# Routing four turns at once in a fused mixer and gated-expert kernel on one core of Trainium2

## The reference, cut to what matters

```python
xn = layernorm(x)                        # 16 sequences x 256 tokens x 128 channels = 4096 tokens
# mixer, per sequence: six projections of x + (prev - x) * mix
state = state * decay + u                # a scan over 256 tokens
mn = groupnorm(r * state)                # 16 groups of 8 channels
s = (mn * gn_w + gn_b) * g @ W_out.T + b_out
# experts: four rounds over the same tokens
for r in range(4):
    logits = cur @ Wg[r] + bg[r]
    vals, idx = top_k(logits, 2);  w = softmax(vals)      # of 4 experts
    y = gelu(cur @ W1[e] + b1[e]) @ W2[e] + b2[e]         # all four experts, 128 -> 512 -> 128
    cur = cur + sum_e cw[e] * y[e]
out = x + s * silu(cur)
```

## Time and profile before

| | us |
|---|---|
| median of 3 runs | 899.56 |
| the profiled execution, its own time | 899.89 |
| its span in the trace | 898.0 |
| TensorE matmul busy | 814.8 (91%) |
| VectorE busy | 808.4 (90%) |
| ScalarE busy | 647.8 (72%) |
| chain that ended last, by engine | PE 49%, DVE 31%, ACT 10%, issue 9%, DMA 1% |

### The profile page before, as it was taken

The page is one execution under the profiler, slowest core; times in us unless marked ns, Lnnn a source line. Parts: engine busy times, 40 slices in busy tenths (PEclk is TensorE's granted clock), DMA queues, the critical chain, the costliest instruction groups (busy, mean ns, idle before and its releaser), DMA issues.

```text
span 898.0 us, 12889 instructions
## 1 busy us (share of the span) xinstructions
PE 814.8 (91%) x3640; PEld 646.8 (72%) x3640; DVE 808.4 (90%) x1756; ACT 647.8 (72%) x900; POOL 146.8 (16%) x167
## 2 busy tenths in 40 slices
PE   3889999889899999999999999999999999898994
PEld 2667777767687777778777777877777787676873
DVE  8899999988989989898998989899898989998894
ACT  3656767767687777768777777877777787676872
POOL 5011241421111111111111111111111111111111
PEclk7799999999999999999999999999999999998997
DMA  7132344323444333334333343433333354533453
GB/s 208 48 82 36 83 89 86 77 44 82 95 88 88 82 54 76 82 94 94 82 82 68 67 86 84 94 82 86 80 60 79 82 118 95 129 58 72 119 118 82
DMA packets 40458, 76.58 MB, mean 85 GB/s; under 512 B 6384, under 2 KB 18800, under 8 KB 36336
## 3 DMA queue, kind: packets, MB, share of 16 engines
q0 software_dynamic: 18432, 33.56, 21.7%
q1 hardware_dynamic: 21808, 42.69, 16.9%
q10 hardware_dynamic: 192, 0.01, 0.0%
HBM read 40.33 MB, written 2.36 MB: 48 GB/s over the span
## 4 chain that ended last, share of the span: by engine, by line
PE 49%; DVE 31%; ACT 10%; issue 9%; DMA 1%; DVEq 0%; ACTq 0%; POOLq 0%
PE h_bank L734 8%; PE h_bank L733 8%; PE h_bank L732 8%; DVE g_lo L517 7%; PE y_bank L765 6%; PE y_bank L770 6%; PE y_bank L766 6%; ACT g L341 6%; ACT g_hi L345 4%; DVE lgt L481 2%; DVE xm L573 2%; DVE xm_lo L581 2%; DVE tmp L528 2%; PE r_bank L742 1%; DVE xm_hi L579 1%
## 5 line engine op out<-in xcount | busy, mean ns | idle before, releaser
L341 ACT ACTIVATE g<-h_bank,b_c 128x512 f32<-128x512 f32 x512 | 333.3, 680 | 126.2 <-PE h_bank L734 121.4
L517 DVE TENSOR_TENSOR g_lo<-g,g_hi 128x1024 fp32r<-128x1024 f32 x256 | 306.7, 1223 | 40.5 <-ACT g_hi L345 37.8
L345 ACT ACTIVATE g_hi<-g 128x1024 fp32r<-128x1024 f32 x256 | 271.6, 1061 | 8.1
L309 POOL DMA_DIRECT2D cur<-tmp x128 | 111.3, 870 | 734.8 <-DVE tmp L528 506.9
L732 PE MATMUL h_bank<-cur_lo,w_hi 128*128 128x512 f32 x512 | 210.3, 411 | 0.0
L733 PE MATMUL h_bank<-cur_hi,w_lo 128*128 128x512 f32 x512 | 207.1, 404 | 0.0
L734 PE MATMUL h_bank<-cur_hi,w_hi 128*128 128x512 f32 x512 | 206.6, 404 | 0.0
L765 PE MATMUL y_bank<-g_hi,w_hi 128*128 128x512 f32 x512 | 203.0, 396 | 0.0
L766 PE MATMUL y_bank<-g_hi,w_lo 128*128 128x512 f32 x512 | 202.2, 395 | 0.0
L770 PE MATMUL y_bank<-g_lo,w_hi 128*128 128x512 f32 x512 | 140.4, 395 | 0.1
L734 PEld LDWEIGHTS h_bank<-cur_hi,w_hi 128*128 128x128 f32 x512 | 99.1, 194 | 24.4
(11 more groups left out here) (110 smaller groups left out, 671.3 us busy)
## 6 DMA issues: line engine op xcount, KB each, us to landing
cw_b<-cw_scratch SPq DMA_DIRECT2D x32, 1024.0 KB, 5.8
cur<-tmp POOLq DMA_DIRECT2D x128, 256.0 KB, 3.3
cur<-in_x SPq DMA_DIRECT2D x8, 256.0 KB, 5.1
xr<-in_x SPq DMA_DIRECT2D x8, 256.0 KB, 6.6
out<-o SPq DMA_DIRECT2D x8, 256.0 KB, 6.0
g<-in_w SPq DMA_DIRECT2D x4, 256.0 KB, 5.4
cw_scratch<-cw SPq DMA_DIRECT2D x32, 8.0 KB, 1.4
cw_b<-in_proj_t SPq DMA_DIRECT2D x1, 384.0 KB, 3.4
```

What stands on the lines that cost most here:

```text
L309: pool.dma_start(cur[:, ds((s // E % NB) * BLK, BLK)], tmp[:, t % 2, :], accum_op=ALU.add).then_inc(summed, DMA)
L341: nc.scalar.activation(g[:, gb, ft * BLK:(ft + 1) * BLK], hb[ft][:, :], ACT.Gelu_apprx_tanh, bias=b1_c[:, e * FT + ft:e * FT + ft + 1]).th ...
L345: nc.scalar.activation(g_hi[:, gb, h], g[:, gb, h], ACT.Copy).then_inc(g_hi_done, 1)
L517: nc.vector.tensor_tensor(g_lo[:, gb, h], g[:, gb, h], as_f32(g_hi[:, gb, h]), ALU.subtract).then_inc(g_lo_done, 1)
```

## The change

- **Router.** Turns 0 to 7 are routed one by one as before. The turns from 8 on are routed four at a time, in passes 3, 5, 7, 9, 11 and 13: `logits_four` runs eight matmuls at t = 4 into all 128 partitions of `r_bank`, two per turn. Its weights are windows of `wg_pad`, which is zero but for 8 columns, so that turn n of the four adds its scores to partitions 32n to 32n + 31 and zeros to the others. One `router_scores` (t = 5) and one `router_gates` (t = 6) then work on 128 partitions. Passes 4, 6, 8, 10, 12, 14 and 15 have no router; pass 3 has one for turn 7 at t = 1 and 2, and the first of four at t = 5 and 6.
- **Splits.** `cur_hi` and `cur_lo` have five buffers. From pass 4 to 13 the splits lie at t = 1 and t = 3, two turns further ahead; pass 3 has four of them; passes 14 and 15 have none. A split now waits for `up_done` of the turn whose buffer it takes.
- **Banks.** The transposes of `mixed` and `mn` go to `p_bank` and wait for `p_empty`.
- **Gates.** The transfer of a turn's gates now waits in the SyncE queue for the last `combine` of the turn before the previous one as well, since the gates of four turns are ready together.
- **Loops.** `Fori` is gone: all passes are written out, and semaphore counts are constants.
- Some buffers are merged (`mixed` with `st`, `gated` with `gn`, `z` with `th`, `xn_st` with `o`), `wg_now` is gone, and two small fills make the zeros of `wg_pad` before pass 0.

```diff
-        cur_hi, cur_lo = sb("cur_hi", [128, 2, BLK], f32r), sb("cur_lo", [128, 2, BLK], f32r)
+        cur_hi, cur_lo = sb("cur_hi", [128, SPLITS, BLK], f32r), sb("cur_lo", [128, SPLITS, BLK], f32r)
...
-        lgt = sb("lgt", [RP, RT, RP])
+        lgt = sb("lgt", [128, RT, RP])
...
+        def routed(i):
+
+            return SPLIT_PASSES <= i <= TAIL_PASS and i % 2 == 1
...
+        def splits_at(i, t):
+
+            if norming(i):
+                return {3: (2 * i + 2,), 7: (2 * i + 3,)}.get(t, ())
+            if i == SPLIT_PASSES:
+                return {1: (2 * i + 2, 2 * i + 3), 3: (2 * i + 4, 2 * i + 5)}.get(t, ())
+            if i <= TAIL_PASS:
+                return {1: (2 * i + 4,), 3: (2 * i + 5,)}.get(t, ())
+            return ()
...
-                sp.wait_ge(cw_ready, k + 1)
+                q, n = k % 2, batch_of(k)
+                row = RP * (k % QUADS if k >= NB else 0)
+                sp.wait_ge(cw_ready, n + 1)
+                if k >= 2:
+                    sp.wait_ge(combined, 2 + E * (k - 1))
...
+            def split_cur(k):
+
+                off, q = k % NB * BLK, k % SPLITS
+                if k >= NB:
+                    dve.wait_ge(summed, DMA * E * (k - NB + 1))
+                if k >= SPLITS:
+                    dve.wait_ge(up_done, E * FT * (k - SPLITS + 1))
...
-            def mixer_norm(i, job):
-
-                dve.wait_ge(r_full, job + 1)
-                m3 = rb[:, 0:2 * D].rearrange("p (g c) -> p g c", c=GW)
+            def mixer_norm(i):
+
+                dve.wait_ge(p_full, JOBS * i + J_MIXED + 1)
+                m3 = pb[:, 0:2 * D].rearrange("p (g c) -> p g c", c=GW)
...
+            def turn_mixer(i, job, src, ready):
+
+                pe.wait_ge(ready, i + 1)
+                pe.wait_ge(p_empty, JOBS * i + job)
+                for t in range(2):
+                    ins = nc.tensor.transpose(pb[:, t * D:(t + 1) * D], src[:, t * D:(t + 1) * D], ident[:, :])
+                ins.then_inc(p_full, 1)
...
+            def logits_four(k, job):
+
+                pe.wait_ge(r_empty, job)
+                for n in range(QUADS):
+                    pe.wait_ge(cur_split, 2 * (k + n + 1))
+                    w = wg_pad[:, WG_AT - RP * n:WG_AT - RP * n + 128]
+                    q = (k + n) % SPLITS
+                    nc.tensor.matmul(rb[:, :], w, cur_lo[:, q, :], start=(n == 0), stop=False)
+                    last = nc.tensor.matmul(rb[:, :], w, cur_hi[:, q, :], start=False, stop=(n == QUADS - 1))
+                last.then_inc(r_full, 1)
```

More of the change, by code:

```diff
@@ L174, in mixer_gated_experts, with norming, ending, kinds_of @@
         GATEW, SMALL, MIXW = 2, 4, 2
[L179 to L182, removed]
-        R_BEFORE = 3
[L184 to L192, removed]
+        J_RW, J_AG, J_KV, J_MIXED, J_MN, J_S = range(6)
+        JOBS = 6
+        def norming(i):
+            return i < SPLIT_PASSES
+        def ending(i):
+            return i >= TAIL_PASS
+        def routed(i):
+            return SPLIT_PASSES <= i <= TAIL_PASS and i % 2 == 1
+        def kinds_of(i):
+            kinds = []
+            if i < SPLIT_PASSES:
+                kinds += ["logits_odd", "norm_even", "logits_even", "norm_odd"]
+            if i == SPLIT_PASSES:
+                kinds += ["logits_odd"]
+            if ending(i):
+                kinds += ["end_even"]
+            if routed(i):
+                kinds += ["logits_four"]
+            if ending(i):
+                kinds += ["end_odd"]
+            if i == PASSES - 1:
+                kinds += ["end_6"]
+            return kinds
+        R_BEFORE = 3
+        r_jobs = {}
+        for i in range(PASSES):
+            for name in kinds_of(i):
+                r_jobs[i, name] = R_BEFORE + len(r_jobs)
+        r_jobs[PASSES - 1, "end_7"] = R_BEFORE + len(r_jobs)
         def end_job(b):
@@ L251, in store @@
                              o[:, b % 2, :].rearrange("p (t d) -> p t d", t=TPB)).then_inc(stored[b % 2], DMA)
[L253 to L256, removed]
+            spread_gates(0)
+            for i in range(TAIL_PASS):
+                spread_gates(2 * i + 1)
+                spread_gates(2 * i + 2)
             for i in range(TAIL_PASS, PASSES):
@@ L404, in _ @@
             act.wait_ge(lo_split, 2 * E)
-            passes(act, one_pass)
+            for i in range(PASSES):
+                one_pass(i)
             end_tanh(NB - 1)
@@ L410, in _ @@
             class Own:
[L412 removed]
+                n = 0
             def link(ins):
@@ L719, in _ @@
[L719 to L722 removed]
+                    if t == 1 and i <= SPLIT_PASSES:
+                        router_scores(2 * i + 1, r_jobs[i, "logits_odd"])
+                    elif t == 2 and i <= SPLIT_PASSES:
+                        router_gates(2 * i + 1)
+                    elif t == 5 and norming(i):
+                        router_scores(2 * i + 2, r_jobs[i, "logits_even"])
+                    elif t == 5 and routed(i):
+                        router_scores(2 * i + 2, r_jobs[i, "logits_four"])
+                    elif t == 6 and (norming(i) or routed(i)):
+                        router_gates(2 * i + 2)
@@ L724, in _ @@
+                    combine(i, t)
+            for i in range(PASSES):
+                one_pass(i)
             end_output(NB - 2, end_job(NB - 2))
-            dve.wait_ge(p_empty, 4 * PASSES)
+            dve.wait_ge(p_empty, JOBS * PASSES)
             end_product(NB - 1)
@@ L837, in _ @@
             pe.wait_ge(lo_split, 2 * E + 2)
-            passes(pe, one_pass)
+            for i in range(PASSES):
+                one_pass(i)
             turn(end_job(NB - 1), z[:, 1, :], TPB, z_ready, NB)
```

335 lines of the change are left out of this document (158 added, 177 removed).

## The result

| | before | after |
|---|---|---|
| median, us | 899.19 (4 runs) | 863.04 (862.53 to 863.11) |
| ratio | | 0.9595 (95%: 0.9576 to 0.9614) |
| profiled execution, us | 899.89 | 862.53 |
| its span, us | 898.0 | 860.7 |
| granted clock, mean | 0.972 | 0.981 |

The change makes the kernel 4% faster. The forecast was 861.7 us. (A fourth execution of the changed kernel took 2798.85 us and is left out of the ratio and the range; the median of all four is the 863.04 above, that of the other three 862.96.)

The account below looks back on a forecast made before the run. TensorE was taken as the bound, less two stalls where VectorE is late (VectorE in passes 0 and 1). Gains 0.2 + 2.4 - 0.8 + 24.9 + 2.4 + 7.8 + 1.3 = 38.2 us off 899.89 gave 861.7; range 852 to 876.

Parts of the forecast that it names:

- pass 3: Pass with both routers and four splits: 52.0 us against 51.2, `xm_lo` stall 1.5 and `go_lo` 1.15, a loss of 0.8.
- passes 4 to 12: Loop passes: even ones 47.9 us, odd ones 50.9 with a 1.15 us `go_lo` wait, 443.1 against 468.0, gain 24.9.
- pass 14: No router there: two stalls of 4.2 us and 2.66 of low clock go, scores save 0.93; 48.7 us, gain 7.8.
- Router on 128 partitions: VectorE's router calls: 128 partitions at the price of 32, up to 1 us more allowed; load falls 7.7 and 3.8 us.
- Wider weight loads: TensorE's score matmuls: 128-column loads of 0.194 us against 0.087 cost nothing, covered by the matmul before.
- The copies to `wg_now` go and two fills come: Passes 0 and 1, bound by VectorE and keeping their routers: a few tenths either way, gain 0.2 us.
- At least 22 us: Gate transfers: start at least 22 us before they are wanted and land within about 8, so cost nothing.
- Loops cost nothing: Loop branches: priced at nothing, as 49.15 us busy and 2.85 of named waits fill a 52.0 us pass.
- A: Rival, odd passes: router chain hidden, six TensorE stalls of 1.15 us go, 853 to 855 us; chance 0.13.
- B: Rival: VectorE late at more places, even passes keep a 1.2 to 2 us stall, 875 to 878 us; chance 0.13.
- C: Rival: straight-code fetch or wider loads cost TensorE 2 us a pass over 16 passes, 890 us; chance 0.07.
- D: Rival: GpSimd's accumulating DMAs pace the steps, slower from 7.0 us each, 947 us at 7.4; chance 0.03.

Follow-up runs that it names:

- the bank alone: Kernel before with only the transposes of `mixed` and `mn` moved to `p_bank`: 887.89 us, ratio 0.9868.
- the unrolled kernel: Kernel before with only its hardware loops written out as straight code: 900.3 us, ratio 1.0009.
- the routing alone: Changed kernel with the transposes of `mixed` and `mn` given back to `r_bank`, all else kept: 874.22 us, ratio 0.9721.
- the late gates: Changed kernel with each transfer of gates held until all four steps of the turn before are combined: 869.09 us, ratio 0.9659.
- the copy given to GpSimd: Changed kernel with router behind gate and bias load in two parts, plus normalised x copied into `cur` by GpSimd in passes 0 to 2: 858.06 us, ratio 0.9548.

## Why the prediction came out right

The forecast was 861.7 us, the median 863.04. By its own terms, from the profiled executions:

| term | predicted gain, us | measured |
|---|---|---|
| what comes before pass 0 | 0 | -1.4 |
| passes 0 and 1 | 0.2 | 0.5 |
| pass 2 | 2.4 | 2.7 |
| pass 3 | -0.8 | -1.2 |
| passes 4 to 12 | 24.9 | 25.2 (467.9 to 442.8) |
| pass 13 | 2.4 | 2.4 |
| pass 14 | 7.8 | 7.8 |
| pass 15 | 1.3 | 1.3 |
| sum | 38.2 | 37.3 |

**Passes 4 to 12.** Even ones were to take 47.9 us and take 47.8; odd ones 50.9 and 50.9. The new wait for `go_lo` was put at 1.15 us and cost 1.16, and moving the router behind the gate removed it (855.13 us). So close a hit has some luck in it: wanted at 353.77 and there at 354.8 is 1.03 us, with the loop's register work 1.2, and 1.15 is a choice between them. That the wait for `lgt` would hand over to `go_lo`, and not simply vanish, was the step on which the sum hung: the bank alone gave 0.8 of the 1.96 us per pass.

**Router on 128 partitions.** It was costed at the price of 32 and took 3.23 against 3.34 us. VectorE's busy time fell by less than forecast, by 6.8 us in even passes and 3.3 in odd ones instead of 7.7 and 3.8 (47.12 to 40.36 and 43.85), because the 3.34 us were a stretch of time with small gaps in it and were taken as busy time. Nothing in the sum hung on it.

**Wider weight loads.** They cost nothing, as taken. TensorE at the scores of turns 12 to 15 in pass 5, with the four matmuls of `down` before them and the next `up` behind:

```profile
334.48 1.09 PE L811 MATMUL y_bank<-g_lo,w_hi 128*128 128x512 f32 x4
335.41 0.40 PE L830 MATMUL r_bank<-cur_lo,wg_pad 128*128 128x512 f32 x1
335.64 0.39 PE L831 MATMUL r_bank<-cur_hi,wg_pad 128*128 128x512 f32 x1
...
337.27 0.39 PE L765 MATMUL h_bank<-cur_lo,w_hi 128*128 128x512 f32 x1
```

Eight of them take 337.27 - 335.41 = 1.86 us, 0.233 each, the pitch of any 512-column matmul here, though each has a load of its own:

```profile
L830 PEld LDWEIGHTS r_bank<-cur_lo,wg_pad 128*128 128x128 f32 x24 | 4.5, 187 | 1.1
```

0.187 us of load against the 0.087 of the narrow ones, all behind the matmul before. The Trainium skill (TensorE: Matmul & The Clock Gate, section LDWEIGHTS) says that a load's time follows its columns, and the same page (section "Step-by-step: what each phase is for") that loads are pulled ahead of running matmuls. The rows agree with the second. Of the first they show the direction and not the proportion: 16 times the columns take about twice as long.

**Pass 14.** The clock is 1.00 there, and the 2.66 us of low clock are gone together with the stall. That the one goes with the other was read from a single place of the trace before, and the pass ahead of it speaks against a fixed link. TensorE behind its waits for `lgt` in passes 13 and 14 of the kernel before:

```profile
767.59 0.41 PE L742 MATMUL r_bank<-ident,mn 128*128 128x128 f32 x2 [3.30 <-DVE lgt L481]
...
821.45 0.66 PE L742 MATMUL r_bank<-ident,mn 128*128 128x128 f32 x2 [3.24 <-DVE lgt L481]
```

The longer stall, in pass 13, kept the clock at 1.00. In pass 14 the grant was 0.99 from 818.2 to 820.5 us and 0.50 from there on, so it fell inside the stall and not behind it. The later windows at 0.97 (passes 3, 8, 12, 13 and 14 of the unrolled kernel, 7 and 13 of the routing alone, 13 and 14 of the bank alone) all have a stall of 1.88 us or more, and no window of the changed kernel from pass 3 on, with stalls of 1.5 us at most, is below 1.00. The reverse doesn't hold: pass 7 of the unrolled kernel has such a stall and keeps its clock, and so does pass 3 of the late gates with a stall of 3.4 us. So without long stalls from pass 3 on no low clock was seen, and with one it may come or not. That the 2.66 us would come back was a good bet on the trace, and not a thing it showed.

**Where a step failed.** "The copies to `wg_now` go and two fills come, a few tenths either way" was the whole of what the prediction said on the start. It left out that the bias load grows from 32 to 128 partitions and lies between the loads that VectorE waits for first: 1.1 us, and 0.25 for the fills. Every DMA that a change widens belongs in the list, however few bytes it has. The prediction followed the transfers of the gates and not those of the start.

"At least 22 us" for the gates was wrong for the turns 8, 12, 16, 20, 24 and 28, which have 10 to 11, and for turns 0 to 7, which have 11 to 15, much as in the kernel before. The term stayed at nothing only because the two transfers, some 7 to 9 us, still fit, once by 1.2 us.

"Loops cost nothing: 49.15 busy and 2.85 of named waits fill the 52.0 us" did not exclude what it meant to exclude. The loop's cost lay inside a named wait: 0.35 us of the 1.23 for `xm_lo` was register work on VectorE. The sum was right all the same, because the change removes that wait whole, and what goes with it can't be gained twice.

**Pass 3** was put at a loss of 0.8 us and lost 1.2: the `xm_lo` wait was taken at 1.5 us and shows 1.5 of idle time, which is 1.65 by starts, and `go_lo` 1.0. The remaining 0.2 us is not traced.

**The rivals.** A is what the router behind the gate gives, and not what the change gives. B (a stall left in even passes) didn't happen: TensorE idles for none of pass 6. C and D didn't either; no wait on `summed` or `cw_b` appears. (C was priced at 890 us; its own 2 us in 16 passes, added to the forecast, come to 894.) The late gates show that a wait on `cw_b` would have been real, at 1.65 us in one turn of two.

## What to carry to other kernels

When a wait is taken away, list the waiting engine's next needs with their times and compare each with when its producer really has it; the gain is the distance to the next late one (0.8 of 1.96 us here for the bank alone), and an order in which the urgent result comes before the patient one (gate before router) can be worth having, here another 7.9 us. Write down every load whose shape grows, even one of 8 KB, and look at what else is being loaded beside it at the start, on other queues too. When work is made ready in batches, look for the member that is wanted first: its lead is the shortest, here 10 us where the others had 28 and more. A delay on an engine without slack shows, and on one with slack it doesn't: the same late gates cost nothing in passes 4 to 12 and 0.5 to 1.9 us in each of passes 0, 1, 3 and 13.

## What was not expected of the hardware

- **A small load can delay a large one.** A broadcast of 8 KB to 128 partitions, issued on another queue, went with a wait of 1.1 to 1.6 us for a 256 KB block, in four of four profiles; with 2 KB to 32 partitions first there was none, in seven of seven.
- **Stalls of nearly the same length have different sequels.** In the kernel before, none of the 1.79 us waits for `lgt` in passes 3 to 12 was followed by a fall of the clock. With 1.88 us, three of the ten were (3, 8 and 12 of the unrolled kernel), by some 3.4 us at 1.2 GHz in the one shown, and with 1.9 us in the routing alone two of its six odd passes. Stalls of 3.3 us (pass 13 before) and 3.4 us (pass 3 with late gates) were followed by none. What decides it, the runs don't tell.
- **VectorE's short operations slow down beside GpSimd's elementwise ones.** At the start of the changed kernel, as of the one before, GpSimd works on 128x512 tiles from 7.79 to 12.71 and again from 13.49 us:

```profile
7.79 4.92 POOL L323 TENSOR_TENSOR w_lo<-g,w_hi 128x512 fp32r<-128x512 f32 x4 [5.85 <-ACT w_hi L359]
```

  VectorE's operations on 128x8 take 1.19 us in those stretches and 0.17 us between them:

```profile
11.55 1.19 DVE L465 SCALAR_TENSOR_TENSOR y<-yt,y 128x8 f32<-128x8 f32 x1
12.77 0.17 DVE L463 TENSOR_TENSOR yt<-y 128x8 f32<-128x8 f32 x1
```

  It is seven times the duration for the same kind of instruction. No run took GpSimd's work away there, so here the cause is read from the times alone. But the copy given to GpSimd added such work elsewhere, and there an operation of the same size went from 0.17 to 0.78 us.
